# A two-layer graph kernel: sums over edges as 32-column products over four column groups, and a second product in two row halves

## The chip, the cores and the metric

The kernel runs on one core of one Trainium2 chip. The metric is the device time of the whole program in microseconds (us), the median of several runs. A single profiled execution gives the trace from which all durations below are read. The engines are named as in the profile: PE (TensorE, matrix products), PEld (its weight loads, which can overlap products), DVE (VectorE), ACT (ScalarE), POOL (GpSimd), SP (SyncE, which here only starts DMAs).

## What is computed

Two message-passing layers over the same graph of 6250 nodes and 200000 edges, the edges sorted by destination. All data is float32. A node has 64 scalars and 32 vectors of three components (160 numbers). Layer 0, cut to what matters (layer 1 adds one more message, `m_v3`, built from a cross product, and has a gate at the end):

```python
weight = silu(edge_length_embedded @ W_fc1) @ W_fc2      # per edge: 192 numbers (layer 1: 224)
gs, gv = x1s[edge_src], x1v[edge_src]                    # gather the source node's row
mid0a = w0 * gs * e_s                                    # 64 scalars
mid0b = w3 * (einsum('euc,ec->eu', gv, e_v) / sqrt3)     # 32 scalars
mid1a = w1[:, :, None] * gs[:, :, None] * e_v[:, None, :]   # 64 vectors
mid1b = w2[:, :, None] * gv * e_s[:, :, None]            # 32 vectors
agg = segment_sum(concat(...), edge_dst, num_segments=n) / sqrt(16)
# then linear mixes of agg per node, a residual and a layer norm
```

## The kernel before

**Tiling.** Edges are padded to 392 groups of 512; a group is four tiles (`TPG`) of 128 edges, one edge on each partition. The program has five stages: `setup_phase` (tables of window starts, scaled weights, node projections), `edge_phase` for layer 0, `layer0_nodes_phase` (50 tiles of 128 nodes), `edge_phase` for layer 1, and `layer1_nodes_phase` (50 tiles). Each edge phase writes out four groups by hand and loops 97 times over a body of four (`GPB`).

**Sums over edges.** Because the edges are sorted, the 512 destinations of a group nearly always lie in a window of 40 nodes (`WIN`). DVE makes `match`, for each edge a row of 40 zeros and a one at its destination; ACT multiplies that row by the edge's attributes, so that there are five rows of 40 for each edge (`which` 0 to 4: times e1, e2, e3, e0, and plain). DVE makes the messages (`msg`, `MW` columns per edge, 96 scalars and vectors per component). PE then multiplies: messages as the stationary operand, a match row as the moving one, and the result, message columns on the partitions and 40 window nodes in the free dimension, is summed in PSUM over the four tiles (`ps_sum`, up to four chunks of 40). DVE adds that window to `sums` in SBUF at the window's start (line 574). A group whose destinations span more than one window runs a loop of extra windows (lines 510 to 515 on PE).

**Who does what in one group.** On PE, the turn for group j is `hid(j)` (line 468, first product of the edge network), `edge_weights(j-1)` (line 479, second product, into `ps_w`) and `sum_group(j-2)` (line 489 in `window_sums`). ACT takes silu of `ps_h` (line 449) and scales the match rows (line 456). DVE runs `messages(j)` (lines 605 to 646), which needs `w_done` of that group and its gathered rows, then `add_group(j-1)`, which needs `sum_done`. POOL gathers the source rows: four indirect DMAs for each group (line 433), each for 128 edges, into four sets of `rows`; the gather of group j waits for the messages of group j-4. SP loads indices, network inputs and attributes, each in pairs of groups, in a fixed order with waits between them (lines 403 to 416).

**The layout that the change touches.** `window_sums` writes products of 64 message columns into partitions 0 to 63 or 64 to 127 and products of 32 columns into partitions 64 to 95 or 96 to 127. Per tile of edges that is, in layer 0, one product of 64 columns against 120 (three match rows), two of 64 against 40, and four of 32 against 40; layer 1 has two more of 64 against 40. PE splits each float32 product into two weight loads and two matmuls. In the placement before, the four groups of 32 partitions get 120, 120, 120 and 200 moving columns per tile in layer 0, and 160, 160, 160 and 240 in layer 1.

**Second product.** In layer 1 `hidden` holds two tiles of edges at once, 64 hidden values of each on partitions 0 to 63 and 64 to 127, and `fc2_1` is block diagonal (480 columns): one product with all 128 rows makes the weights of two tiles.

**Node phases.** `sums` is staged by ACT (lines 758, 892) and multiplied by `out0` or `out1`, whose columns repeat and zero-pad the weights to fit the mixed layout (lines 788 to 790 and 925 to 928). The order of work on each engine is as written; nothing is reordered by a planner.

## Time and profile before

| | us |
|---|---|
| median of 3 runs | 4755.46 |
| lowest, highest | 4745.83, 4756.82 |
| the profiled execution, from first to last instruction (its span) | 4749.6 |

In the span, setup takes until about 138 us, the edges of layer 0 until about 2165, the nodes of layer 0 until about 2387, the edges of layer 1 until about 4611, and the nodes of layer 1 the rest. The difference between span and median, 5.9 us, lies around the profiled instructions. A timeline row is one or several consecutive instructions, with the start of the first and the time until the end of the last; a row's end on PE is modelled, so a duration is best read from one row's start to the next row's start.

### The profile page before, as it was taken

The page shows a single profiled execution, that of the slowest core. Times are in us where ns is not written, and L with a number is a line of the kernel's source. Part 1 is how long each engine was busy: PE and PEld are TensorE (multiplying, and loading weights), DVE is VectorE, ACT ScalarE, POOL GpSimd, SP SyncE. Part 2 cuts the span into 40 slices and gives each one's busy share as a digit, 9 for nine tenths or more (in the row PEclk, how much of TensorE's full clock was granted, in tenths as well). Part 3 has the DMA queues.
Part 4 walks back from the last instruction along what each step waited for, and adds up shares of the span by engine and source line. Part 5 has one row for each costly group of instructions (what it writes and reads, how often), then busy time and mean ns, then how long its engine had stood idle before and what let it go on. Part 6 is the DMA issues. An engine that isn't in the chain of part 4 may idle for free. (4 is left out here: it accounts for less than half of the span.)

```text
span 4749.6 us, 166762 instructions
## 1 busy us (share of the span) xinstructions
PE 4615.8 (97%) x58000; PEld 3438.2 (72%) x58001; DVE 2968.4 (62%) x7746; ACT 2970.1 (63%) x12216; POOL 3050.4 (64%) x3215
## 2 busy tenths in 40 slices
PE   7899999999999999999889999999999999999996
PEld 4677777777777777776667777777777777777766
DVE  3455545454455445455767777777777777777768
ACT  1566666666666666663366676767676766666653
POOL 2677777777777777771266666666666666666641
PEclk9999999999999999999899999999999999999995
DMA  3222222222222222223343333333333333333333
GB/s 104 71 71 71 70 71 70 71 70 71 71 71 71 70 71 70 72 70 91 90 129 108 106 108 107 108 107 107 108 107 108 106 108 106 108 107 108 106 89 96
DMA packets 356348, 430.11 MB, mean 91 GB/s; under 512 B 203298, under 2 KB 248648, under 8 KB 356112
## 3 DMA queue, kind: packets, MB, share of 16 engines
q0 software_dynamic: 156288, 329.79, 25.4%
q1 hardware_dynamic: 199618, 98.11, 8.0%
q10 hardware_dynamic: 400, 1.68, 0.1%
q8 instruction: 23, 0.38, 0.0%
q14 instruction: 19, 0.16, 0.0%
HBM read 405.56 MB, written 23.74 MB: 90 GB/s over the span
## 5 line engine op out<-in xcount | busy, mean ns | idle before, releaser
L433 POOL DMA_INDIRECT e_rows<-scratch_table,e_index x3136 | 2963.7, 945 | 1305.2 <-issue 1209.6
L456 ACT ACTIVATE e_match<-e_match,e_attr 128x40 f32<-128x40 f32 x10976 | 2481.3, 315 | 237.7 <-DMA e_attr<-in_edge_attr 230.2
L489 PEld LDWEIGHTS e_sum<-e_match,e_msg 128*64 128x64 f32 (+1 forms) x50176 | 2102.4, 124 | 653.8 <-issue 363.7
L489 PE MATMUL e_sum<-e_match,e_msg 128*32 128x40 f32 (+2 forms) x50176 | 2486.3, 228 | 0.2 <-issue 0.2
L479 PE MATMUL e_w<-k_fc,e_hidden 100*128 100x192 f32 (+1 forms) x4704 | 1273.8, 407 | 0.0
L449 ACT ACTIVATE e_hidden<-e_h 100x512 f32<-100x512 f32 (+1 forms) x784 | 384.1, 490 | 1170.3 <-PE e_h L468 1170.2
L479 PEld LDWEIGHTS e_w<-k_fc,e_hidden 100*128 100x128 f32 (+1 forms) x4704 | 832.9, 191 | 384.4 <-issue 364.0
L574 DVE TENSOR_TENSOR sums<-sums,e_sum 128x120 f32 (+1 forms) x784 | 235.9, 301 | 947.9 <-PE e_sum L489 884.3
L635 DVE TENSOR_TENSOR e_msg<-e_w,e_rows 128x512 f32<-128x512 f32 x784 | 540.7, 690 | 451.3 <-PE e_w L479 437.5
L468 PE MATMUL e_h<-e_inputs,k_fc 128*100 128x512 f32 (+1 forms) x1568 | 709.9, 534 | 30.5 <-DMA e_inputs<-in_inputs 26.9
L641 DVE TENSOR_TENSOR e_msg<-e_w,e_rows 128x384 f32<-128x384 f32 x784 | 428.4, 546 | 0.0
L643 DVE TENSOR_TENSOR e_msg<-e_w,e_rows 128x384 f32<-128x384 f32 x784 | 428.1, 546 | 0.0
L554 DVE TENSOR_TENSOR e_match<-e_misc,e_dst_rel 128x160 f32<-128x160 f32 x788 | 252.4, 320 | 53.0 <-DMA e_dst_rel<-scratch_dst_rel 11.2
L468 PEld LDWEIGHTS e_h<-e_inputs,k_fc 128*100 128x100 f32 (+1 forms) x1568 | 216.2, 177 | 74.6 <-DMA e_inputs<-in_inputs 27.3
L625 DVE TENSOR_TENSOR e_misc<-e_misc,e_rows 128x384 f32<-128x384 f32 x392 | 218.0, 556 | 5.0 <-DMA e_rows<-scratch_table,e_index 4.5
L626 DVE TENSOR_TENSOR e_cross_b<-e_misc,e_rows 128x384 f32<-128x384 f32 x392 | 214.5, 547 | 0.0
L640 DVE TENSOR_TENSOR e_msg<-e_misc,e_cross_b 128x384 f32<-128x384 f32 x392 | 214.0, 546 | 0.0
L646 DVE TENSOR_TENSOR e_msg<-e_w,e_msg 128x384 f32<-128x384 f32 x392 | 213.6, 545 | 0.0
L605 DVE COPY e_misc<-e_attr 128x48 f32<-128x48 f32 x392 | 82.5, 211 | 134.3 <-issue 115.1
L618 DVE TENSOR_TENSOR e_match<-e_misc,e_match 128x160 f32<-128x160 f32 x392 | 124.2, 317 | 2.0 <-DVE e_match L554 0.2
L729 POOL DMA_DIRECT2D m_xv<-in_xT_v x10 | 5.4, 540 | 156.2 <-DVE m_y L822 140.3
L758 ACT ACTIVATE m_staged<-sums 128x384 f32 (+1 forms) x50 | 26.0, 523 | 86.9 <-PE m_agg L790 77.7
(122 smaller groups left out, 1440.8 us busy)
## 6 DMA issues: line engine op xcount, KB each, us to landing
e_rows<-scratch_table,e_index POOLq DMA_INDIRECT x3136
e_inputs<-in_inputs SPq DMA_DIRECT2D x196, 256.0 KB
e_attr<-in_edge_attr SPq DMA_DIRECT2D x392, 24.0 KB, 1.7
e_inputs<-in_inputs SPq DMA_DIRECT2D x196, 40.0 KB
e_index<-in_src SPq DMA_DIRECT2D x392, 4.0 KB, 1.9
scratch_self<-m_h SPq DMA_DIRECT2D x10, 480.0 KB, 4.7
f_self<-scratch_self POOLq DMA_DIRECT2D x10, 480.0 KB, 5.2
m_xrow<-in_x POOLq DMA_DIRECT2D x10, 400.0 KB, 4.9
```

What stands on the lines that cost most here:

```text
L433: pool.indirect_dma_start(out=rows[j][:, t, :], out_offset=None, in_=table_dram, in_offset=bass.IndirectOffsetOnAxis(ap=index[q][:, c:c + ...
L449: nc.scalar.activation(hidden[j % 2][:, :], ps_h[0:layer.hid, 0:layer.group_cols], ACT.Silu, scale=layer.silu_scale).then_inc(silu_done, 1)
L456: last = nc.scalar.activation(match[j][:, t, c, :], match[j][:, t, 4, :], ACT.Copy, scale=attr[q][:, e0 + t, e:e + 1])
L468: nc.tensor.matmul(ps_h[0:layer.hid, 0:n], w[f"fc1_{L}"][:, :], inputs[j // 2][:, (j % 2) * n:(j % 2) * n + n], start=True, stop=True).the ...
L479: last = nc.tensor.matmul(ps_w[j % 2][:, c0:c0 + n], hidden[j % 2][:, u * P:(u + 1) * P], w[f"fc2_{L}"][:, :], start=True, stop=True)
L489: return nc.tensor.matmul(out[rows, c0:c0 + n, :], m[:, t, f:f + rows.stop - rows.start], m5[:, t, which:which + n, :], start=(first and t ...
L554: return nc.vector.tensor_tensor(into[:, :, 4, :], iota_t, rel_of(g).unsqueeze(2).broadcast_to([P, TPG, WIN]), ALU.is_equal)
L574: nc.vector.tensor_tensor(at, at, window, ALU.add).then_inc(added, 1)
L625: nc.vector.tensor_tensor(comps(cross_a), e3(3), comps(r[:, :, 96:192]), ALU.mult)
L635: nc.vector.tensor_tensor(m[:, :, 0:128].rearrange("p t (k n) -> p t k n", k=2), wt[:, :, 0:128].rearrange("p t (k n) -> p t k n", k=2), r ...
L641: nc.vector.tensor_tensor(comps(m[:, :, 128:224]), w_v(128), comps(r[:, :, 64:160]), ALU.mult)
L643: last = nc.vector.tensor_tensor(comps(m[:, :, 224:320]), w_v(160), comps(r[:, :, 64:160]), ALU.mult)
```

## The change

- `window_sums` now makes only products of 32 message columns, 10 per tile in layer 0 and 13 in layer 1, on a layout in which each chunk of `sums` holds one vector component (chunks 0 to 2) or the scalars (chunk 3). The moving columns per group of 32 partitions and tile become 160, 160, 120, 120 in layer 0 and 160, 160, 160, 200 in layer 1. `first` is set on one product per partition group only. In layer 0, DVE zeroes `ps_sum` once, and PE waits for that.
- Both layers use all four chunks, so layer 0's window add is 160 wide instead of 120, its staging 512 instead of 384, and the clearing of `sums` after layer 0 covers four chunks instead of three.
- The second product of layer 1 is four products of 64 rows by 224 columns instead of two of 128 rows by 480; `inputs1` is laid out so that the two row halves write different PSUM banks.
- `out0` and `out1` lose the padding: layer 0's nodes use three products of 64 columns and one of 128 (before 320, 128 and 192), layer 1's three of 32 and one of 96 (before 192, 64, 128 and 96). Setup has fewer products and scalings, and the five warm-up products per edge phase have 224 columns instead of 480.

```diff
@@ edge_weights
+                fc2, n = w[f"fc2_{L}"], layer.wn
                 for u in range(TPG // layer.tiles_per_product):
-                    c0, n = u * layer.tiles_per_product * WPITCH, w[f"fc2_{L}"].shape[1]
-                    last = nc.tensor.matmul(ps_w[j % 2][:, c0:c0 + n], hidden[j % 2][:, u * P:(u + 1) * P], w[f"fc2_{L}"][:, :],
-                                            start=True, stop=True)
+                    for h in range(layer.tiles_per_product):
+                        c0, k = (u + 2 * h) * WPITCH, fc2.shape[0] // layer.tiles_per_product
+                        last = nc.tensor.matmul(ps_w[j % 2][:, c0:c0 + n], hidden[j % 2][k * h:k * h + k, u * P:(u + 1) * P],
+                                                fc2[k * h:k * h + k, :], start=True, stop=True)
@@ window_sums
-                    product(slice(0, 64), 0, 64, 0, n=3, first=True, end=(L == 0))
-                    product(slice(64, 128), 2, 0, 3, first=True)
-                    product(slice(64, 128), 0, 128, 3)
-                    product(slice(64, 96), 1, 192, 3, end=(L == 0))
-                    for c in range(3):
-                        last = product(slice(96, 128), 1, 224 + V * c, c, end=(L == 0 and c == 2))
-                    if L == 1:
-                        product(slice(0, 64), 3, 320, 4, end=True)
-                        last = product(slice(64, 128), 3, 384, 4, end=True)
+                    product(0, 0, 64, 0, n=3, first=True)
+                    product(1, 0, 96, 0, n=3, first=True)
+                    product(2, 0, 128, 3, first=True)
+                    product(3, 3, 224, 0, first=True)
+                    product(2, 1, 160, 3)
+                    product(3, 3, 256, 1)
+                    product(0, 3, 0, 3, end=True)
+                    product(1, 3, 32, 3, end=True)
+                    if L == 0:
+                        product(2, 2, 192, 3, end=True)
+                        last = product(3, 3, 288, 2, end=True)
+                    else:
+                        product(2, 2, 192, 3)
+                        product(3, 0, 320, 4)
+                        product(2, 3, 288, 2, end=True)
+                        product(3, 1, 352, 4)
+                        last = product(3, 2, 384, 4, end=True)
@@ add_group
-                window = ps_sum[j % 2][:, 0:layer.chunks, :]
+                window = ps_sum[j % 2]
...
-                at = sums[:, 0:layer.chunks, bass.ds(start, WIN)]
+                at = sums[:, :, bass.ds(start, WIN)]
@@ layer 0 nodes, output
-                nc.tensor.matmul(agg, staged[b][:, 1, :], w["out0"][:, 0:320], start=True, stop=False)
-                nc.tensor.matmul(agg[:, :, 0:64], staged[b][:, 0, :], w["out0"][:, 320:448], start=False, stop=False)
-                nc.tensor.matmul(agg[:, :, 64:160], staged[b][:, 2, :], w["out0"][:, 448:640], start=False,
-                                 stop=True).then_inc(out_mm, 1)
+                for c in range(3):
+                    nc.tensor.matmul(agg[:, :, V * c:V * c + V], staged[b][0:MID, c, :], w["out0"][0:MID, 0:2 * V], start=True, stop=True)
+                nc.tensor.matmul(agg[:, :, V3:D], staged[b][:, 3, :], w["out0"][:, 2 * V:192], start=True, stop=True).then_inc(out_mm, 1)
```

How it stands on PE. In layer 1, one group, before (`e_h` is `hid`, `e_w` is `edge_weights`, `e_sum` is `window_sums`; a shape is output partitions by columns; the first two tiles of the four):

```order
L468 MATMUL e_h<-e_inputs,k_fc_1 128x256
L479 MATMUL e_w<-k_fc_1,e_hidden 128x480 x2
L505 TENSOR_LOAD k_table
L505 ISA x2
L489 MATMUL e_sum<-e_match,e_msg 64x120
L489 MATMUL e_sum<-e_match,e_msg 64x40 x2
L489 MATMUL e_sum<-e_match,e_msg 32x40 x4
L489 MATMUL e_sum<-e_match,e_msg 64x40 x2
L489 MATMUL e_sum<-e_match,e_msg 64x120
L489 MATMUL e_sum<-e_match,e_msg 64x40 x2
L489 MATMUL e_sum<-e_match,e_msg 32x40 x4
```

and now:

```order
L440 MATMUL e_h<-e_inputs,k_fc_1 128x256
L453 MATMUL e_w<-k_fc_1,e_hidden 128x224 x4
L487 TENSOR_LOAD k_table
L487 ISA x2
L463 MATMUL e_sum<-e_match,e_msg 32x120 x2
L463 MATMUL e_sum<-e_match,e_msg 32x40 x11
L463 MATMUL e_sum<-e_match,e_msg 32x120 x2
L463 MATMUL e_sum<-e_match,e_msg 32x40 x11
```

The turn keeps its order; the sums no longer alternate between 64 and 32 columns, and have 52 products per group where they had 36. In layer 0 they have 40 where they had 28.

At the start of layer 0's nodes, two node tiles before (`m_self` is the residual part, `m_agg` the part from `sums`):

```order
L785 MATMUL m_self<-k_node_v,m_xv 128x2x96
L786 MATMUL m_self<-k_node_s,m_xs 128x2x64
L788 MATMUL m_agg<-k_out,m_staged 128x320
L789 MATMUL m_agg<-k_out,m_staged 128x2x64
L790 MATMUL m_agg<-k_out,m_staged 128x2x96
L785 MATMUL m_self<-k_node_v,m_xv 128x2x96
```

and now:

```order
L770 MATMUL m_self<-k_node_v,m_xv 128x2x96
L771 MATMUL m_self<-k_node_s,m_xs 128x2x64
L774 MATMUL m_agg<-k_out,m_staged 128x2x32 x3
L775 MATMUL m_agg<-k_out,m_staged 128x2x64
L770 MATMUL m_self<-k_node_v,m_xv 128x2x96
```

Three products became four, with half the columns in all (320 for 640).

## Rows read from the trace of the kernel before

**Rows 1.** A stretch: length; busy us (instructions) of PE, PEld, DVE, ACT, POOL; clock, DMA.
```profile
3600.00:4000.00 400.00, 400.00 (x5538) 284.83 (x5538) 297.98 (x710) 279.86 (x1211) 268.04 (x284) 1.00 0.39 107
```

**Rows 2.** Timeline of PE, layer 0: start, us, instructions, count.
```profile
1504.59 1.47 PE L479 MATMUL e_w<-k_fc,e_hidden 100*128 100x192 f32 x8
1505.98 2.87 PE L489 MATMUL e_sum<-e_match,e_msg 128*64 128x120 f32 x56
1508.78 0.67 PE L468 MATMUL e_h<-e_inputs,k_fc 128*100 128x512 f32 x1
```

**Rows 3.** Timeline of PE, layer 1.
```profile
3000.06 0.70 PE L468 MATMUL e_h<-e_inputs,k_fc 128*128 128x256 f32 x2
3000.60 1.77 PE L479 MATMUL e_w<-k_fc,e_hidden 128*128 128x480 f32 x4
3002.30 3.47 PE L489 MATMUL e_sum<-e_match,e_msg 128*64 128x120 f32 x72
3005.70 0.70 PE L468 MATMUL e_h<-e_inputs,k_fc 128*128 128x256 f32 x2
```

**Rows 4.** Line 433 by phase: count, ns min/median/max, first to last start.
```profile
L433 POOL DMA_INDIRECT e_rows<-scratch_table,e_index x1568: 940/946/1020, 138.4 to 2148.2; - x196
L433 POOL DMA_INDIRECT e_rows<-scratch_table,e_index x1568: 940/946/1010, 2389.3 to 4590.8; - x196
```

**Rows 5.** Timeline of POOL, layer 1: in brackets the idle time before.
```profile
3006.34 0.95 POOL L433 DMA_INDIRECT e_rows<-scratch_table,e_index  x1 [0.30 <-issue]
3007.59 0.95 POOL L433 DMA_INDIRECT e_rows<-scratch_table,e_index  x1 [0.30 <-issue]
```

**Rows 6.** Stretches, weight loads of line 489 alone, one layer-1 tile: length, busy (count).
```profile
3003.00:3003.43 0.43, 0.43 (x10) 1.00 1.01 363
3003.43:3003.47 0.04, 0.00 (x0) 1.00 0.95 378
3003.48:3003.77 0.29, 0.28 (x8) 1.00 0.74 269
```

**Rows 7.** The page, groups of instructions: count, busy us, mean ns, idle before.
```profile
L489 PE MATMUL e_sum<-e_match,e_msg 128*32 128x40 f32 (+2 forms) x50176 | 2486.3, 228 | 0.2 <-issue 0.2
```

**Rows 8.** Timeline of DVE, layer 1, two groups.
```profile
3000.43 0.32 DVE L574 TENSOR_TENSOR sums<-sums,e_sum 128x160 f32 x1 [1.11 <-PE e_sum L489]
...
3004.41 0.54 DVE L646 TENSOR_TENSOR e_msg<-e_w,e_msg 128x384 f32<-128x384 f32 x1
3006.07 0.32 DVE L574 TENSOR_TENSOR sums<-sums,e_sum 128x160 f32 x1 [1.11 <-PE e_sum L489]
...
3010.37 0.55 DVE L646 TENSOR_TENSOR e_msg<-e_w,e_msg 128x384 f32<-128x384 f32 x1
```

**Rows 9.** Timeline of DVE: the last window add of each edge phase.
```profile
2163.76 0.28 DVE L574 TENSOR_TENSOR sums<-sums,e_sum 128x120 f32 x1 [2.67 <-PE e_sum L489]
...
4610.12 0.32 DVE L574 TENSOR_TENSOR sums<-sums,e_sum 128x160 f32 x1 [3.11 <-PE e_sum L489]
```

**Rows 10.** Timelines of PE and of DVE, nodes of layer 0.
```profile
2282.03 0.81 PE L788 MATMUL m_agg<-k_out,m_staged 128*128 128x320 f32 x2
...
2285.41 0.81 PE L788 MATMUL m_agg<-k_out,m_staged 128*128 128x320 f32 x2
...
2280.37 0.38 DVE L822 SCALAR_TENSOR_TENSOR m_y<-m_self,k_attr,m_xrow 128x160 f32<-128x160 f32 x1
...
2283.55 0.38 DVE L822 SCALAR_TENSOR_TENSOR m_y<-m_self,k_attr,m_xrow 128x160 f32<-128x160 f32 x1
```

**Rows 11.** A stretch in the nodes of layer 1, columns as in rows 1.
```profile
4620.00:4700.00 80.00, 69.03 (x284) 62.23 (x282) 65.86 (x309) 30.63 (x102) 11.28 (x13) 0.61 0.23 68
```

**Rows 12.** Timeline of PE as layer 1's edges begin.
```profile
2391.82 1.22 PE L468 MATMUL e_h<-e_inputs,k_fc 128*128 128x256 f32 x2 [0.47 <-ACT e_hidden L449]
```

**Rows 13.** The page: an instruction queue (packets, MB); the index loads (last: landing).
```profile
q8 instruction: 23, 0.38, 0.0%
...
e_index<-in_src SPq DMA_DIRECT2D x392, 4.0 KB, 1.9
```

More of the change, by code:

```diff
@@ L62 @@
 WPITCH = 256
-MW = 448
+MW = 416
 WARM_UP = 5
@@ L246, in _ @@
             pe.wait_ge(l_in, 32)
-            for c in range(16):
-                vec = c not in (6, 7, 14, 15)
-                col = OUT0_COLUMNS[c] + (64 if c >= 12 else 0)
-                n = V if vec else S
-                last = nc.tensor.matmul(ps_out[:, col:col + n], l2[:, c, :], l3[:, S:S + V] if vec else l3[:, 0:S],
-                                        start=True, stop=True)
+            for k in range(2):
+                nc.tensor.matmul(ps_out[:, V * k:V * k + V], l2[:, k, :], l3[:, S:S + V], start=True, stop=True)
+            for k in range(2):
+                c0 = 2 * V + S * k
+                last = nc.tensor.matmul(ps_out[:, c0:c0 + S], l2[:, 2 + k, :], l3[:, 0:S], start=True, stop=True)
             last.then_inc(out0_done, 1)
@@ L487, in window_sums, with product @@
                 for t in range(TPG):
-                    def product(rows, c0, f, which, n=1, first=False, end=False):
-                        return nc.tensor.matmul(out[rows, c0:c0 + n, :], m[:, t, f:f + rows.stop - rows.start],
+                    def product(g, c0, f, which, n=1, first=False, end=False):
+                        return nc.tensor.matmul(out[32 * g:32 * g + 32, c0:c0 + n, :], m[:, t, f:f + 32],
                                                 m5[:, t, which:which + n, :], start=(first and t == 0),
                                                 stop=(end and t == TPG - 1))
-                    product(slice(0, 64), 0, 64, 0, n=3, first=True, end=(L == 0))
-                    product(slice(64, 128), 2, 0, 3, first=True)
-                    product(slice(64, 128), 0, 128, 3)
-                    product(slice(64, 96), 1, 192, 3, end=(L == 0))
-                    for c in range(3):
-                        last = product(slice(96, 128), 1, 224 + V * c, c, end=(L == 0 and c == 2))
-                    if L == 1:
-                        product(slice(0, 64), 3, 320, 4, end=True)
-                        last = product(slice(64, 128), 3, 384, 4, end=True)
+                    product(0, 0, 64, 0, n=3, first=True)
[15 more added lines that the diff above has]
+                        last = product(3, 2, 384, 4, end=True)
                 return last
@@ L524, in _ @@
             for c in range(WARM_UP):
-                nc.tensor.matmul(ps_h[:, 0:480], w["ident"][:, :], w["out1"][:, :], start=True, stop=True)
+                nc.tensor.matmul(ps_h[:, 0:224], w["ident"][:, :], w["fc2_1"][:, :], start=True, stop=True)
             with pe.Fori(1, BODIES) as i:
@@ L539, in _ @@
                     nc.vector.memset(inputs[q][:, :], 0.0).then_inc(zeroed, 1)
-            for b in range(2):
-                nc.vector.memset(msg[b][:, :, 416:448], 0.0)
+            if L == 0:
+                for b in range(2):
+                    nc.vector.memset(ps_sum[b], 0.0).then_inc(zeroed, 1)
             nc.vector.memset(dst_rel[:, T:T + AHEAD * TPG], 0.0)
@@ L592, in add_group @@
                             skip_runtime_bounds_check_because="extras count the whole windows up to a destination below NPAD")
-                        at = sums[:, 0:layer.chunks, bass.ds(there, WIN)]
+                        at = sums[:, :, bass.ds(there, WIN)]
                         nc.vector.tensor_tensor(at, at, window, ALU.add).then_inc(x_added, 1)
@@ L681, in layer0_nodes_phase @@
         h1 = [sb(f"h1_{s}", [P, TPU, R1]) for s in range(UPB)]
-        staged = [sb(f"staged{b}", [P, 3, P]) for b in range(2)]
+        staged = [sb(f"staged{b}", [P, 4, P]) for b in range(2)]
         y = [[sb(f"y{b}_{c}", [P, D]) for c in range(4)] for b in range(2)]
@@ L733, in _ @@
             pool.wait_ge(stage_done, NT)
-            nc.gpsimd.memset(sums[:, 0:3, :], 0.0)
+            nc.gpsimd.memset(sums[:, :, :], 0.0)
         @block.sync
@@ L757, in stage @@
                 at_least(act, out_mm, n - 1)
-                nc.scalar.activation(staged[b][:, :, :], sums[:, 0:3, bass.ds(n * P, P)], ACT.Copy).then_inc(stage_done, 1)
+                nc.scalar.activation(staged[b][:, :, :], sums[:, :, bass.ds(n * P, P)], ACT.Copy).then_inc(stage_done, 1)
             def deviation(n, i, s, k, b):
@@ L924, in output @@
                 o = ps[b]
-                nc.tensor.matmul(o[:, 0:O1], staged[b][:, 1, :], w["out1"][:, 0:192], start=True, stop=False)
-                nc.tensor.matmul(o[:, 0:64], staged[b][:, 0, :], w["out1"][:, 192:256], start=False, stop=False)
-                nc.tensor.matmul(o[:, 64:O1], staged[b][:, 2, :], w["out1"][:, 256:384], start=False, stop=False)
-                nc.tensor.matmul(o[:, 0:V3], staged[b][:, 3, :], w["out1"][:, 384:480], start=False, stop=True).then_inc(out_mm, 1)
+                for c in range(3):
+                    nc.tensor.matmul(o[:, V * c:V * c + V], staged[b][:, c, :], w["out1"][:, 0:V], start=True, stop=True)
+                nc.tensor.matmul(o[:, V3:O1], staged[b][:, 3, :], w["out1"][:, V:V + S1], start=True, stop=True).then_inc(out_mm, 1)
             node_loop(pe, output)
```

51 lines of the change are left out of this document (19 added, 32 removed).

## The prediction, made before the changed kernel ran

> **What bounds the kernel now.** I read the busy times by stretch first, then the timelines of PE and POOL, then who waits. In both edge phases PE never rests: in 400 us of layer 1 it is busy for 400, while DVE has 298, ACT 280 and POOL 268 [rows 1]. The edge phases are what counts: from the first gather to the last window add they take 2163.8 - 138.4 and 4610.1 - 2389.3, together 4246 of the 4750 us [rows 4, 9]. One group on PE takes, in layer 0, 1.39 for the second product, 2.80 for the sums and the rest of 5.13, 0.94, for the first [rows 2, 4]; in layer 1 it is 0.54, 1.70 and 3.40, so 5.64 [rows 3]. The next limit stands close behind. Where POOL has nothing to wait for, its gathers start 1.25 us apart (0.95 of work, 0.30 of issue) [rows 5], and a group has four: 5.00 us. The gathers of one phase run from 138.4 to 2148.2 and from 2389.3 to 4590.8 [rows 4]; over 1567 steps of one gather that is 5.13 and 5.62 per group, so PE holds POOL back by 0.13 and 0.62. A gain on PE beyond these two amounts is not seen in the time. There are no extra windows on this data: 50176 matmuls on line 489 are 392 x (56 + 72) exactly [rows 2, 3, 7].
>
> **The sums.** The change takes away the alternation of 64 and 32 columns and adds products: 40 for 28 in layer 0, 52 for 36 in layer 1, two matmuls each. Is a product of 32 columns beside others in other column groups nearly free, or does it queue? The price of a moving column comes from the second product of layer 1: 4 matmuls of 480 columns in 1.70 us, 0.885 ns each [rows 3]. The stretch of one tile in layer 1 begins with ten loads for matmuls of 280 x 2 = 560 columns in 64-column form, and 0.48 us after its start the first load of the 32-column form begins [rows 6]. One after another these columns would take 0.496 us, with no time for the first load or the 0.04 in which nothing is loaded. So products on the two halves of the columns do run side by side. If they do fully, the columns explain only (160 + 120) x 2 x 0.885 = 0.50 of a tile's 0.85 us in layer 1 and 0.42 of 0.70 in layer 0: the other 0.28 to 0.35 lies at the two changes of form in each tile, where the array empties and the first weights load uncovered. Those go.
>
> Ends for the new sums. Low: four groups side by side, bounded by the fullest: 160 columns x 2 x 0.885 x 4 tiles = 1.13 in layer 0 and 200 in its place, 1.42, in layer 1, plus 0.1 to enter. High: no two ever overlap and each matmul follows at the pace of the eight loads of 32 columns, 0.29 / 8 = 0.036 [rows 6]: 80 x 0.036 = 2.9 and 104 x 0.036 = 3.8. Between them, with two groups side by side as the row shows, (560 x 2 x 0.885 x 4) / 2 = 1.98 and (680 x ...) / 2 = 2.41. I take 2.0 and 2.4, since two abreast is what a row shows and four is only the same thing carried on.
>
> A rule speaks against products this small. The Trainium skill, "TensorEngine Tiling (Array Packing)", section "Instruction Overhead", says that a matmul costs about 60 cycles whatever its columns, so that one should not cut a dimension that is already small; "TensorE: Matmul & The Clock Gate" puts the floor at 25 ns from start to start. By that the sums would be 2.0 and 2.6 us, and the low end could not be reached; no row here goes below 36 ns over a run of eight. The time forecast would be the same.
>
> **The second product of layer 1.** 2 products of 480 columns become 4 of 224. Serially: 8 matmuls x 224 x 0.885 = 1.59; if the row halves run side by side, 0.80. No row shows two row halves at once, so both ends stay, each with one change of form, 0.1 to 0.2. I take 1.3. Nobody downstream minds: DVE waits for w_done once per group.
>
> **PE after the change.** Layer 0: 0.94 + 1.39 + 2.0 = 4.3 (3.6 to 5.2). Layer 1: 0.54 + 1.3 + 2.4 = 4.2 (2.9 to 5.9). Both centres lie below POOL's 5.00, so **POOL becomes the bound** in both layers. What then is late next? DVE in layer 1: from one window add to the end of line 646 is 4.52 without the attribute copies (3000.43 to 3004.95, a 0.32 wait for PE in it) and 4.85 with them (3006.07 to 3010.92) [rows 8], 4.7 in the mean, and some 0.2 to pass from the last message to the next add: 4.9 at most, under 5.00 by little. ACT has 280 of 400 us at 5.63 per group, 3.9 [rows 1]. The add in layer 0 grows by a third to the 0.32 of layer 1 [rows 8, 9], under slack. SP's loads wait for gathers, first products and sums of groups long past; with POOL as the bound the sums of a group end some two turns after its gather, and the indices were asked for before that, so I cost its order at nothing. It has about one pair of groups of cover.
>
> **The sum.** Gathers of layer 0: 1567 x 1.25 = 1958.8 for 2009.8: -51.0. Layer 1: 1958.8 for 2201.5: -242.7. Tails from the last gather's start to the last add: before 15.6 and 19.3, because POOL was groups ahead [rows 4, 9]. Now POOL is last, and what follows it is its own 0.95, the landing, one group of messages and one of sums: I estimate 9 and 10.5, so -7 and -9. Nodes of layer 0: a turn is 3.38 on PE and 3.18 on DVE [rows 10]; the new products have half the columns, so at most DVE's 3.18 is reached, 50 x 0.2 = 10 at best, nothing at worst (four products need two more loads of 128 columns); I take -5. ACT's wider staging and POOL's longer clearing lie beside the stores that end that phase. Nodes of layer 1: DVE is busy for 66 of 80 us and PE waits for ACT, so 0 [rows 11]. Setup loses seven short scalings: -1. Total -316. Against the profiled execution: 4749.6 - 316 = 4434. The median of the runs stands 5.9 above that span, so **4440 us**, 6.6% faster.
>
> **Rivals.**
>
> *Column groups do not overlap as I think* (the slower side). If all products ran in sequence, column by column, the sums would be 560 x 2 x 0.885 x 4 = 3.97 and 4.81: PE at 6.30 and, with the serial second product, 6.94 per group, or 392 x (1.17 + 1.32) = +980, 5730 us. Against it: the 0.48 us for 560 columns [rows 6]. At the pace of one matmul per 0.036 instead, PE has 5.2 and 5.1 to 5.9: 4550 to 4900. It decides where the two groups together pass 5.13 + 5.62. Chance 0.03 each.
>
> *The loop no longer stays in PE's instruction store* (slower too). The trace: one instruction queue brought 23 packets, 0.38 MB, in the whole run [rows 13], though each edge loop ran 97 times; so the loops were not fetched again. Counting two loads and two matmuls per product and the copy of the sums for extra windows, layer 1's loop body grows from 4 x (3 + 72) x 4 = 1200 to 4 x (5 + 104) x 4 = 1744 instructions, beside a few dozen of control, half as much again, and nothing shows that this still fits. The Trainium skill, "Runtime: NRT & Kernel Launch", section "Instruction fetch mechanics", says that TensorE's store holds 2048 instructions in blocks of 256 and that a taken branch to a block that is not there waits for a DMA. By that the new body, some 1800 instructions in eight or nine blocks, just fits or just doesn't. The price from this kernel: the 23 packets are 16.5 KB each, the whole program, so the body of layer 1 was some 5 of them and is now some 7. No row prices a packet that is waited for; the nearest is the landing of a small load, 1.9 us [rows 13]. One per body, at the jump back, is 0.5 per group, and PE's 4.2 hides it under 5.00. All seven, waited for every time, would be 7 x 1.9 / 4 = 3.3 per group: PE at 7.5 in layer 1, 4440 + 392 x 2.5 = 5420. Against no change it decides at 5.9 per group, 1.7 us of fetching. Chance of that 0.04.
>
> *The clock.* PE will rest for 15 to 30% of each turn. Through the edge phases the granted clock is 1.00 with PE always busy [rows 1]; in the nodes of layer 1, where PE stands before 11 of 80 us and works in short bursts, it is 0.61, mostly the 1.2 GHz level [rows 11]. At that level the first product of layer 1 takes 1.22 for 0.70 [rows 12, 3]; all of PE's 4.2 would be about 7. That would at once make PE busy without rest, as now, so it can't last; a third of the time low gives 5.1 per group on average, +40 to +80: 4500. Chance 0.10.
>
> *DVE and PE hand over late in layer 1.* DVE's 4.9 is near 5.00; with one wait of 0.3 for PE per group it binds at 5.2: +80, 4520. It speaks against this that w_done and the sums come a turn ahead once PE is faster. Chance 0.10.
>
> *Sums bound as before because the layout gains nothing*: then layer 0 stays, and layer 1 gains its second product alone, 392 x 0.4: 4600. Chance 0.02.
>
> **How the numbers follow.** Forecast 0.68, clock 0.10, DVE 0.10, the rest 0.12. A measurement of this kernel tells 0.3%, 14 us, from no change. Slower by more: 0.08 (serial, fetch, and part of the 0.036 case); within: 0.01; faster: 0.91. The low end: POOL's 5.00 is firm, tails and nodes can give 15 more: 4422. The high end takes in the clock and DVE cases: 4550.
>
> **What would show it.** In the trace after: gathers 1.25 apart throughout, last starts near 2097 and 4285; POOL the engine without idle time, PE with waits for DVE of 0.5 to 1.5 per group; sums of line 463 in 1.2 to 2.6 us with no gap between loads inside a group; second product between 0.8 and 1.7; granted clock 1.00; instruction packets near 31, not thousands. Wrong would be: gathers further apart than 1.25 with DVE or PE as the releaser, or a clock below 1 in the loops.

## The result, and the profile after

The changed kernel takes **5733.9 us** (median of 4 runs, 5727.5 to 5736.8) beside 4752.9 for the kernel before in the same session: a ratio of 1.206, 95% interval 1.204 to 1.208. It is 20.6% slower, where 6.6% faster was forecast. Its profiled execution has a span of 5729.4 us.

The page of the kernel after shows in three lines where to look: busy time by engine, the clock in 40 slices, and an instruction queue (packets, MB, share).

```profile
PE 3761.5 (66%) x81596; PEld 2835.8 (49%) x81597; DVE 2912.3 (51%) x7737; ACT 2951.2 (52%) x12216; POOL 3055.4 (53%) x3215
...
PEclk9999999999999985577777777777777777777775
...
q8 instruction: 895, 14.66, 1.1%
```

PE works less than before in all (3761.5 us busy for 4615.8), and yet every engine waits. The queue that had brought 23 packets [rows 13] brings 895. The gathers by phase (line 405 is line 433 of before) say when:

```profile
L405 POOL DMA_INDIRECT e_rows<-scratch_table,e_index x1568: 942/946/1020, 136.9 to 2095.1; - x196
L405 POOL DMA_INDIRECT e_rows<-scratch_table,e_index x1568: 940/946/1005, 2423.0 to 5562.3; - x196
```

Layer 0 went from 2009.8 us to 1958.2, as forecast. Layer 1 went from 2201.5 to 3139.3, which is 8.01 us per group in place of 5.62 [rows 4]. PE's timeline over one turn of layer 1's loop (four groups), from one first product to the same one of the next turn:

```profile
4002.03 1.22 PE L440 MATMUL e_h<-e_inputs,k_fc 128*128 128x256 f32 x2 [9.11 <-issue]
4003.18 1.87 PE L453 MATMUL e_w<-k_fc,e_hidden 64*128 64x224 f32 x8
4004.97 2.89 PE L463 MATMUL e_sum<-e_match,e_msg 128*32 128x120 f32 x104
4009.93 0.69 PE L440 MATMUL e_h<-e_inputs,k_fc 128*128 128x256 f32 x2 [2.06 <-issue]
...
4017.27 1.76 PE L463 MATMUL e_sum<-e_match,e_msg 128*32 128x40 f32 x96 [0.70 <-issue]
4021.39 0.97 PE L440 MATMUL e_h<-e_inputs,k_fc 128*128 128x256 f32 x2 [2.36 <-issue]
...
4034.38 1.22 PE L440 MATMUL e_h<-e_inputs,k_fc 128*128 128x256 f32 x2 [8.18 <-issue]
```

Each gap in brackets is put down to "issue": PE waits for nothing that another engine or a transfer of data would release. The products themselves are short. The DMA queues of 32 us of the same stretch show what arrives meanwhile, nine packets in one turn:

```profile
q8 instruction: 9, 0.15, 2.2%
```

With the same stretches as before, layer 0, the node stage and layer 1 (columns as in rows 1):

```profile
1500.00:1900.00 400.00, 305.76 (x7229) 231.06 (x7220) 195.19 (x563) 260.02 (x1044) 302.47 (x320) 1.00 0.28 73
2140.00:2360.00 220.00, 220.00 (x757) 170.10 (x756) 98.80 (x337) 60.19 (x189) 13.95 (x21) 0.50 0.26 73
3600.00:4000.00 400.00, 218.61 (x5586) 163.01 (x5586) 205.46 (x494) 191.74 (x836) 189.63 (x202) 0.75 0.30 80
```

In layer 1 PE is busy for 219 of 400 us, against 400 of 400 [rows 1]. It rests for 14.5 of each turn's 32 us; shared out over the nine packets that is 1.6 us each in the mean. That the rests are waits for these packets is inferred here, and tested below. The second line holds another loss: in the node stage after layer 0 the clock is 0.50, its 1.2 GHz level, and PE never rests, while in the middle of that stage before it had

```profile
2190.00:2370.00 180.00, 159.54 (x791) 117.91 (x791) 129.48 (x400) 65.42 (x220) 32.14 (x25) 0.90 0.38 105
```

The sum by phase, in us, read from the gathers and the spans (e1 and e16 are the experiments of that number; the forecast column has the predicted differences from before, and -12 is -7 for the tail of layer 0's edges and -5 for the nodes):

| | before | after | e1 | e16 | forecast |
|---|---|---|---|---|---|
| to the first gather | 138.4 | 136.9 | 136.7 | 136.9 | -1 |
| gathers of layer 0 | 2009.8 | 1958.2 | 1958.7 | 1958.9 | -51.0 |
| to the next first gather (nodes) | 241.1 | 327.9 | 327.7 | 242.9 | -12 |
| gathers of layer 1 | 2201.5 | 3139.3 | 1958.6 | 1958.6 | -242.7 |
| to the end | 158.8 | 167.1 | 151.9 | 152.1 | -9 |
| span | 4749.6 | 5729.4 | 4533.6 | 4449.4 | -316, to 4434 |

### The profile page after: what moved, and what is told of

It reads as the page before. It is cut to its first block and busy times, and to the rows that moved or that the text cites. A ratio compares the mean times of both kernels' runs of the same rounds, so it can differ in the third digit from the quotient of the medians.

```text
span 5729.4 us, 213946 instructions
## 1 busy us (share of the span) xinstructions
PE 3761.5 (66%) x81596; PEld 2835.8 (49%) x81597; DVE 2912.3 (51%) x7737; ACT 2951.2 (52%) x12216; POOL 3055.4 (53%) x3215
## 3 DMA queue, kind: packets, MB, share of 16 engines
q8 instruction: 895, 14.66, 1.1%
## 5 line engine op out<-in xcount | busy, mean ns | idle before, releaser
L463 PE MATMUL e_sum<-e_match,e_msg 128*32 128x40 f32 (+1 forms) x72128 | 1454.6, 234 | 518.5 <-DVE e_msg L628 389.0
L463 PEld LDWEIGHTS e_sum<-e_match,e_msg 128*32 128x32 f32 x72128 | 1310.2, 123 | 844.8 <-issue 426.6
L440 PE MATMUL e_h<-e_inputs,k_fc 128*100 128x512 f32 (+1 forms) x1568 | 794.6, 593 | 1349.0 <-issue 1298.1
L453 PE MATMUL e_w<-k_fc,e_hidden 100*128 100x192 f32 (+1 forms) x6272 | 1155.4, 415 | 3.1 <-issue 3.1
L453 PEld LDWEIGHTS e_w<-k_fc,e_hidden 100*128 100x128 f32 (+1 forms) x6272 | 904.7, 223 | 397.8 <-issue 384.5
L440 PEld LDWEIGHTS e_h<-e_inputs,k_fc 128*100 128x100 f32 (+1 forms) x1568 | 250.5, 203 | 1442.5 <-issue 1405.6
L559 DVE TENSOR_TENSOR sums<-sums,e_sum 128x160 f32 x784 | 246.3, 314 | 140.9 <-PE e_sum L463 132.6
L743 ACT ACTIVATE m_staged<-sums 128x512 f32 (+1 forms) x50 | 31.4, 629 | 156.3 <-PE m_agg L775 140.4
```

What stands on the lines that cost most here:

```text
L440: nc.tensor.matmul(ps_h[0:layer.hid, 0:n], w[f"fc1_{L}"][:, :], inputs[j // 2][:, (j % 2) * n:(j % 2) * n + n], start=True, stop=True).the ...
L453: last = nc.tensor.matmul(ps_w[j % 2][:, c0:c0 + n], hidden[j % 2][k * h:k * h + k, u * P:(u + 1) * P], fc2[k * h:k * h + k, :], start=Tru ...
L463: return nc.tensor.matmul(out[32 * g:32 * g + 32, c0:c0 + n, :], m[:, t, f:f + 32], m5[:, t, which:which + n, :], start=(first and t == 0) ...
L559: nc.vector.tensor_tensor(at, at, window, ALU.add).then_inc(added, 1)
```

## The experiments

**Theory A:** layer 1's loop on PE no longer fits into the engine's instruction store, so all of it is fetched again in every turn. Counted in the programs, with four instructions for a 32-bit product, its body has 1276 instructions before and 1820 after; nearly half is the copy of the sums for windows beyond the 40 nodes, which stands in every group and never runs on this data. All instruction counts below are made in this way and come from no trace; blocks are the 256 instructions of the rule that the prediction quotes, and one packet of the queue is 14.66 MB / 895 = 16.4 KB. **Theory B:** the products of 32 columns, or the handover between PE and DVE, are slow in layer 1's mix.

**e1_compact** shortens what is not executed, and **e2_before_padded** lengthens it in the kernel before.

```diff
-                    with pe.Fori(0, extras) as x:
-                        pe.wait_ge(x_matched, before + x + 1)
-                        window_sums(j, match_x).then_inc(x_sum_done, 1)
+                    with pe.Fori(0, extras * TPG) as x:
+                        pe.wait_ge(x_matched, before * TPG + x + 1)
+                        window_sums(j, msg_t, match_t, 1).then_inc(x_sum_done, 1)
```

> The changed kernel with one thing rewritten: the branch for destinations beyond the 40-node window (never taken on this data) holds the products of one tile in place of four, with a loop around them and a VectorE copy of the tile in front. What is executed on this data stays the same. PE's loop body in layer 1 falls from 1820 instructions to 1196 (before the change: 1276), counting four for a product of 32-bit data. Theory A, the loop no longer fits into PE's instruction store: the instruction queue has fewer than 60 packets, not 895, and layer 1 goes at POOL's 5.00 us per group, so that 3139 us between its first and last gather become about 1965 and the total is 5734 - 1175 = about 4560 us (4530 to 4640). Rival B, the 32-column products or the handover of data between PE and VectorE are what costs 8.0 us per group: the branch isn't executed, and the time stays at 5734 (5700 to 5760).

Measured: **4536.0 us** (4534.9 to 4536.4), ratio 0.955 (0.953 to 0.956). Packets, gathers of layer 1, and two turns of PE:

```profile
q8 instruction: 22, 0.36, 0.0%
```
```profile
L406 POOL DMA_INDIRECT e_rows<-scratch_table,e_index x1568: 942/946/1010, 2423.1 to 4381.7; - x196
```
```profile
3500.29 0.69 PE L441 MATMUL e_h<-e_inputs,k_fc 128*128 128x256 f32 x2 [0.51 <-issue]
3500.91 1.03 PE L454 MATMUL e_w<-k_fc,e_hidden 64*128 64x224 f32 x8
3503.18 1.65 PE L462 MATMUL e_sum<-e_match,e_msg 128*32 128x120 f32 x104 [1.25 <-DVE e_msg L634]
3504.85 0.69 PE L441 MATMUL e_h<-e_inputs,k_fc 128*128 128x256 f32 x2
```

The executed products are the same, and the time is 1198 us less. Layer 1 runs at POOL's 5.00 us per group, and PE waits for DVE in each group, as the forecast had it. Theory B is gone: the products of 32 columns and their handover are all still there.

e2 adds to each of the four branches of layer 1's loop in the kernel before:

```diff
                 with pe.If(extras):
+                    for _ in range(34):
+                        nc.tensor.matmul(ps_sum[j % 2][0:64, 3, :], msg[j % 2][:, 0, 320:384], match[j][:, 0, 4, :],
+                                         start=True, stop=True)
```

> The kernel before the change, with 34 products (136 instructions) added inside each of the four never-taken branches of layer 1's loop on PE, so that its body has 1820 instructions like the changed one, in place of 1276. Nothing more is executed. Theory A (instruction store): some 9 packets of instructions per loop body, near 900 in all, and layer 1 at 7.2 to 9.2 us per group in place of 5.62, so 4753 + 388 x 2.4 = about 5680 us (5350 to 6150). Rival B (the new products or the new handover): the padding is never executed, 4753 us (4735 to 4770).

Measured: **6072.9 us**, ratio 1.278 (1.276 to 1.280), 889 packets, and layer 1 at 8.98 us per group:

```profile
q8 instruction: 889, 14.57, 1.1%
```
```profile
L433 POOL DMA_INDIRECT e_rows<-scratch_table,e_index x1568: 940/946/1010, 2395.9 to 5915.6; - x196
```

Instructions that never run cost the old kernel 28%. The central estimate was too low (5680), the bounds held. A group has 2.5 us of rest (PE stands before line 468 for 112.2 us in the stretch from 3600 to 4000), and its products take 6.5 us in place of 5.6, since the clock there is 0.83 where it was 1.00 [rows 1].

**e3_one_gap** asks whether the length of the loop counts or the blocks it touches; the padding is that of e2, 206 products in a single branch of e1.

> e1_compact with 206 products (824 instructions) added inside one of the four never-taken branches of layer 1's loop: the body is 2020 instructions long, longer than the changed kernel's 1820, but 886 of them are passed by in one jump, so that PE touches 6 blocks of 256 instructions, and 8 with the block behind each stretch. Theory A1, what counts is the blocks that are fetched: it fits, under 60 packets, and the time is that of e1_compact. Theory A2, what counts is the length of the loop from its first to its last instruction: about 9 packets per body and 8 us per group or more, 5650 us or more.

Measured: 4536.5 us, 23 packets. A body of 2020 instructions, longer than the changed kernel's 1820, costs nothing when 886 of them are jumped over at once. So the distance from the first to the last instruction doesn't decide; this fits with what was expected if only the blocks that PE passes through, and the one behind each such stretch, are fetched.

**e5_fits, e6_shifted, e9_shifted_again, e14_shifted_healthy** look for the edge. e5 pads e1 by 29 products in each branch; e6 is e5 with 33 more ahead of the loop:

```diff
+            if L == 1:
+                never = pe.value_load(w["table"][0:1, 0:1, 1:2], min_val=0, max_val=NPAD // WIN - 1)
+                with pe.If(never):
+                    for _ in range(33):
+                        nc.tensor.matmul(ps_h[:, 0:224], w["ident"][:, :], w["fc2_1"][:, :], start=True, stop=True)
```

> e1_compact with 29 products (116 instructions) added inside each of the four never-taken branches of layer 1's loop: the body has 1660 instructions and reaches over 7 blocks of 256 instructions (8 with the one fetched behind it). Theory A, nine blocks per turn of the loop don't fit and eight do: under 60 instruction packets, the time of e1_compact, 4536 us (4525 to 4550). Rival A3, the store holds fewer (or the time grows with each instruction that is passed by): between 4600 and 5700 us.

> e5_fits with 33 products more in another never-taken branch ahead of layer 1's loop, which is passed once: the loop is the same 1660 instructions, but begins 137 instructions later, so that it reaches over 8 blocks of 256 (9 with the one behind). Theory A: near 900 instruction packets, and layer 1 at 7.5 us per group or more, 5500 us or more, for the same body as e5_fits. Rival A4, only the length of the body counts: the time of e5_fits, 4536 us.

> The kernel of e6_shifted once more, beside a kernel before that runs at its 4750 us: 1660 instructions per turn of layer 1's loop, 137 of padding passed once ahead of it, so that the loop reaches over 8 blocks of 256 instructions in place of 7. Theory A: near 900 instruction packets again (888 in e6_shifted, 24 in e5_fits), layer 1 at 7.2 us per group or more, and 5400 us or more. Rival A4, the packets come ahead of need and cost little: within 100 us of e1_compact's 4536.

> The kernel of e6_shifted (layer 1's loop of 1660 instructions, begun 137 later than in e5_fits, so that it reaches over 8 blocks of 256), on another chip. Theory A: near 888 instruction packets as in its two runs so far, layer 1 at 7.2 us per group or more, 5400 us or more beside a kernel before at 4750 us. Rival A4: the packets come ahead of need where PE gets its instructions in time otherwise, within 100 us of 4536.

The chip of e5 to e8 and that of e9 to e12 ran the kernel before itself in 8083 and 8078 us, so times from these eight are only set against runs of the same chip. Measured there: e5 7861.5 us with 24 packets, e6 8354.4 us with 888; e9 8345.2 us with 888. The packets answer the question: the same 1660 instructions per turn, begun 137 later, change 24 packets into 888, and on the same chip the time grows by 6.3%. On a chip with the kernel before at 4753 us the shifted kernel takes **5693.1 us** (ratio 1.198, 1.195 to 1.200):

```profile
q8 instruction: 888, 14.55, 1.2%
```
```profile
L406 POOL DMA_INDIRECT e_rows<-scratch_table,e_index x1568: 940/946/1010, 2422.3 to 5525.2; - x196
```

So the price is a step. By the count, a turn of the loop that reaches over seven blocks, eight with the one fetched behind them, runs free; where it reaches over eight, nine with that one, all nine come again. The packets agree to the last one: by the same count the whole programs have 31 full blocks after the change, 25 in e2 and 24 in e14 (23 in the kernel before and 22 in e1, as their queues brought), and 895 - 31, 889 - 25 and 888 - 24 are each 864, nine for each of the 96 jumps back of the 97 turns. Where exactly seven blocks end depends on the hand count; that a shift by 137 instructions makes the difference does not. e5's own time on a chip at 4753 us was not run; e1 and e3, with as few packets, stand for it.

**e15_halves_healthy** (first run as e8_halves_alone and e11_halves_alone) does one part alone in the kernel before; **e18_layout_alone** does the other: e1 with this edit taken back.

```diff
-                    last = nc.tensor.matmul(ps_w[j % 2][:, c0:c0 + n], hidden[j % 2][:, u * P:(u + 1) * P], w[f"fc2_{L}"][:, :],
-                                            start=True, stop=True)
+                    for h in range(layer.tiles_per_product):
+                        c0, k = (u + 2 * h) * WPITCH, fc2.shape[0] // layer.tiles_per_product
+                        last = nc.tensor.matmul(ps_w[j % 2][:, c0:c0 + n], hidden[j % 2][k * h:k * h + k, u * P:(u + 1) * P],
+                                                fc2[k * h:k * h + k, :], start=True, stop=True)
```

> The kernel before the change with the second product of layer 1 in two row halves alone; the sums and everything behind them stay as they were. In e1_compact the eight half products take 1.03 us per group, against 1.70 before [rows 3]. PE's turn in layer 1 of 5.62 us then falls to 4.95, just under POOL's 5.00 per group: layer 1 at 5.00, and 4752 - 392 x 0.62 = about 4510 us (4500 to 4545). Rival: the halves save less beside the old sums, PE stays last and the time is between 4545 and 4650 us; layer 0 is as before in either case.

> The kernel of e8_halves_alone once more, beside a kernel before that runs at its 4750 us: the kernel before with the second product of layer 1 in two row halves alone. In e1_compact the eight half products take 1.03 us per group against 1.70 before [rows 3]: PE's turn in layer 1 falls to 4.95 us, under POOL's 5.00, and the total to 4752 - 392 x 0.62 = about 4510 us (4500 to 4545). Rival: the halves save less beside the old sums, PE stays last in layer 1, 4545 to 4650 us.

> The kernel of e8_halves_alone (before, with the second product of layer 1 in two row halves alone), on another chip. PE's turn in layer 1 falls by 1.70 - 1.03 us to 4.95, under POOL's 5.00 per group: 4752 - 392 x 0.62 = about 4510 us (4500 to 4545). Rival: the halves save less beside the old sums, 4545 to 4650 us.

> e1_compact with the second product of layer 1 as it was before the change (one product for two tiles, against a block-diagonal 128 x 480), so that only the layout of the sums is new, in a loop that fits. PE's turn in layer 1 is then 0.62 + 1.70 [rows 3] + 1.7 for the sums = 4.0 us, under POOL's 5.00: 4536 us as e1_compact (4520 to 4550). Rival: the two parts need each other, and layer 1 stands above 5.1 us per group: 4575 us or more.

Measured: e15 **4510.7 us** (ratio 0.948, 0.947 to 0.950), e18 **4535.8 us** (0.954, 0.953 to 0.956). e15's PE timeline:

```profile
3503.52 0.70 PE L467 MATMUL e_h<-e_inputs,k_fc 128*128 128x256 f32 x2
3504.15 1.03 PE L480 MATMUL e_w<-k_fc,e_hidden 64*128 64x224 f32 x8
3505.11 3.47 PE L490 MATMUL e_sum<-e_match,e_msg 128*64 128x120 f32 x72
3508.51 0.70 PE L467 MATMUL e_h<-e_inputs,k_fc 128*128 128x256 f32 x2
```

A turn is 4.99 us, and the second product takes 0.96 from start to start where it took 1.70 [rows 3]. Either part alone brings layer 1 to POOL's pace, e15 with PE still busy without rest; the change did both. e15 stands below e1 and e18 in the total because it keeps the old node stage after layer 0 (247.8 us from last to first gather for e1's 327.7); layer 0 itself gains only by the new layout (2009.5 in e15, 1958.7 in e1). On the two chips at 8080 us the halves alone were 1.9% and 2.0% slower than before (8240.4 and 8232.2 us), a sign that does not carry over and that was not followed up.

**The node stage after layer 0.** e1 leaves one term of the forecast open, 87 us here. In it the three products of 64 columns on 96 rows (and one of 128) have taken the place of three of 320, 128 and 192, and the clock stays at 0.50. Seven kernels, each with its edit on top of e1:

```diff
 e4:
-                    nc.tensor.matmul(agg[:, :, V * c:V * c + V], staged[b][0:MID, c, :], w["out0"][0:MID, 0:2 * V], start=True, stop=True)
+                    nc.tensor.matmul(agg[:, :, V * c:V * c + V], staged[b][:, c, :], w["out0"][:, 0:2 * V], start=True, stop=True)
 e7, e13, e16, e17, ahead of the stage:
+            for _ in range(24):
+                nc.tensor.matmul(ps_next[1][:, 0:224], w["ident"][:, :], w["fc2_1"][:, :], start=True, stop=True)
 e10 and e13 once, e12 twice before a tile's transposes; e16 once, e17 twice before its first product on the staged sums:
+                    nc.tensor.matmul(ps_tr[b][:, 0:384], w["ident"][0:V3, :], w["node_v0"][:, :], start=True, stop=True)
```

> e1_compact with the three 64-column products of the node stage after layer 0 taken over all 128 rows of the staged tile in place of 96 (the 32 more rows are zeros, the sum is unchanged). The stage took 328 us between layer 0's last and layer 1's first gather against 241 before, at a granted clock of 0.50 against 0.80 to 1.00. Theory C, the number of rows in use decides whether the clock is raised: clock near 1.00 in the stage, 241 to 260 us for it, 70 to 85 us less than e1_compact. Rival D, it is the columns per time (many products of 64 columns, of which each takes longer than its columns): the rows change nothing, clock 0.50 and the time of e1_compact within 5 us.

> e1_compact with 24 unused products of 128 x 224 on PE ahead of the node stage after layer 0, so that its first real products find PE at the full clock. Theory E, the stage holds the full clock once it has it: the stage's clock is 1.00 and it takes 240 to 260 us in place of 328, the total 4536 - 75 = about 4460 us (4445 to 4480). Rival F, with its mix of products the stage falls back to 0.50 of the clock by itself: no gain, and up to 15 us more for the unused products, 4530 to 4555 us.

> e1_compact with one unused product of 128 x 384 per node tile in the node stage after layer 0, on top of its fourteen. In e7_warm_nodes the stage lost the full clock again 10 to 15 us after it had it, with PE busy throughout, so that the mix is suspected: a tile of it has 640 columns in 3.36 us in its first six products at the low clock, against 960 columns in 3.95 us before. Theory G, a product of many columns per tile brings the clock back: 1.00 in the stage, 240 to 262 us for it in place of 328, and 4536 - 75 = about 4460 us (4445 to 4480). Rival H, the stage stays at 0.50 and pays for the products, 50 times 1.3 us: about 4600 us (4580 to 4620).

> As e10_dense_nodes with two such unused products per tile. Theory G: if one was not enough, two are; if one was, the second costs nothing as long as VectorE is what the stage waits for at the full clock: 4460 us (4445 to 4490). Rival H: 0.50 and 50 times 2.6 us more than e1_compact, about 4665 us (4630 to 4690).

> e1_compact with both aids in the node stage after layer 0: 24 unused products of 128 x 224 ahead of it and one unused product of 128 x 384 per tile. e7_warm_nodes alone lost the full clock after 10 to 15 us, e10_dense_nodes never got it, e12_dense_twice got it after 30 us and kept it. Theory G (a tile's columns decide, and fewer are enough to keep the clock than to raise it): 1.00 of the clock from the stage's first tiles on, the stage 245 to 265 us in place of 328, and 4536 - 72 = about 4465 us (4450 to 4485). Rival H: one per tile doesn't keep it, the stage falls to 0.50 and takes 395 to 410 us as in e10: about 4610 us.

> e1_compact with 24 unused products of 128 x 224 ahead of the node stage after layer 0 and one unused product of 128 x 384 in the first step of each tile (in e13 it stood in a later step, so that the first tiles of the stage went without it). Theory G: the full clock stays from the first tile on, the stage takes 245 to 265 us in place of 328, 4536 - 72 = about 4465 us (4450 to 4485). Rival H: one wide product per tile is too little at the full clock as well, the stage falls to 0.50 and takes 400 us: about 4605 us.

> As e16_wide_first with two such products per tile. In e12 a tile took 4.44 us with two of them at the full clock, so 50 tiles take 222 us, and with filling and draining the stage takes about 255: 4536 - 73 = about 4463 us (4450 to 4490) if the clock holds. If it falls all the same, e12 shows that it comes back after some 30 us: 4480 to 4500.

| | last to first gather, us | total, us | beside before at |
|---|---|---|---|
| e1 | 327.7 | 4536.0 | 4751 |
| e4 | 327.5 | 4535.7 | 4751 |
| e7 | 338.5 | 7883.2 | 8083 |
| e10 | 401.8 | 7943.4 | 8078 |
| e12 | 296.2 | 7826.9 | 8078 |
| e13 | 386.8 | 4597.0 | 4753 |
| e16 | 242.9 | **4451.1** | 4752 |
| e17 | 274.4 | 4482.7 | 4752 |

e7, e10 and e12 ran on the two chips at 8080 us; there the same stage without any aid takes 340.0 (e5, the chip of e7) and 340.6 us (e9, the chip of e10 and e12). The rows used are indifferent (e4). In e7 the stage gets the full clock from the products ahead of it and has lost it within 10 us. PE had just rested twice, 0.32 us for DVE and 0.79 for ACT; from then on it is busy without rest, and the clock does not come back:

```profile
3795.00:3805.00 10.00, 10.00 (x57) 9.65 (x56) 0.00 (x0) 0.19 (x1) 3.60 (x6) 1.00 0.65 166
3815.00:3950.00 135.00, 135.00 (x467) 104.59 (x466) 64.47 (x221) 37.12 (x118) 9.98 (x15) 0.50 0.28 78
```

In e10 one wide product per tile leaves the clock at 0.50 throughout. In e12 two per tile raise it by themselves (0.50 from 3780 to 3800, 1.00 from 3820 on, PE busy all the time) and keep it. In e13 the stage starts at the full clock, but its first tiles, while the pipeline fills, go without the wide product; after a rest of 0.32 us for DVE at 2122.4 the clock falls, and it is 0.50 for good. e16 has the same number of unused products with the wide one in each tile's first step, and keeps the clock:

```profile
2120.00:2140.00 20.00, 20.00 (x116) 15.00 (x115) 17.79 (x63) 8.80 (x23) 2.00 (x3) 1.00 0.23 61
2140.00:2360.00 220.00, 191.08 (x1228) 142.86 (x1229) 143.66 (x427) 87.91 (x297) 51.67 (x39) 0.89 0.38 108
```

In every 20 us from 2140 to 2300 of e16 the clock is 1.00 and PE is busy throughout; the 0.89 comes from the end of the stage, behind the last products. The stage is within 2 us of its old 241, and e16 is the fastest kernel of the study: 0.936 of before (0.935 to 0.938). e17's second product only adds work for PE. That the half clock is what costs the 87 us is shown: with more products than e1 and the full clock the stage is back at its old length. Why the clock holds or falls is not settled. The width of the products is one candidate, and for e7 and e13 against e16 there is another that no run separates from it: the rest just before the fall, which e16, with more for PE to do per tile, doesn't have in its first tiles.

## Why the prediction was wrong

**The failed step is the instruction-store rival: an overflow was taken to cost one packet or so per turn, and all of them at every turn was given 0.04.** The prediction named this mechanism, counted the body at 1744 instructions "beside a few dozen of control", and said that some 1800, "in eight or nine blocks, just fits or just doesn't". Then it priced the same body as 7 packets, showed that one per turn would be hidden, and gave no reason for the small chance of the rest. The runs show no such mild case: the packets are nine per jump back or none (888 in all in e6, 24 in e5), and layer 1 takes 8.01 us per group in place of the forecast 5.00. The count could have said more beforehand: 1820 instructions are more than seven times 256, so the body reaches over at least eight blocks wherever it begins, while the body of before, 1276, reached over six, and no row showed that more than that run free. The rule that was quoted, the Trainium skill, "Runtime: NRT & Kernel Launch", section "Instruction fetch mechanics", has 2048 instructions in blocks of 256, eight blocks; by the count, e5 and e14 agree with that (eight blocks with the one behind run free, nine don't). By that rule alone the forecast should have been near an even chance between 4440 and its rival.

**The rival's own price was too low.** It had 7 packets of 1.9 us, 3.3 us per group, on top of a PE turn of 4.2: 7.5, 5420 us. Measured are 9 packets of 1.6 us of rest, 3.6 per group, and a PE that is busy for 4.4 per group in place of e1's 3.5, at a clock of 0.75 in place of 0.97: 8.0 and 5734 us. The two blocks too few are the eighth and the one fetched behind, and the lower clock was not in the price at all.

**The sums** were taken as two abreast, 2.0 and 2.4 us. They take 1.4 (layer 0: 1504.55 to 1505.95 in the trace after) and 1.67 from start to start in e1's layer 1, near the low ends of 1.13 + 0.1 and 1.42 + 0.1. One after another the columns of layer 1 are 4.81 us; in 1.67 us that is 2.9 abreast in the mean, so more than two groups of columns run together. The row that was held to show two abreast showed a lower bound. That is 104 matmuls in 1.67 us, 16 ns each. As an estimate from the pages, the Trainium skill's floor of 25 ns from start to start ("TensorE: Matmul & The Clock Gate", section "Wait — 56ns, not 53.3ns?") and the Trainium skill's 60 cycles per matmul ("TensorEngine Tiling (Array Packing)", section "Instruction Overhead") would make it 2.6 us; where page and row differ, the row decides. **The second product** takes 0.96 to 1.03, not 1.3 and far from the serial 1.59, so two row halves do run side by side.

**POOL as the bound** held: 5.00 us per group in layer 0 after the change and in both layers of e1, 1958.2 to 1958.9 us for the forecast 1958.8. **DVE** was not late: e1's gathers stay 1.25 apart through layer 1. **The tail** after layer 1 was right once the loop fitted (-6.9 for -9). That a gain on PE past POOL's pace is not seen in the time was right too: e15 and e18 have half of the change each and layer 1 at the same 5.00.

**The node stage** was costed at -5 from the turns at full clock [rows 10], with "half the columns" as a gain. With the tail before it, where -12 was forecast, +87 was measured, since the clock was an input of that sum and the change moved it. The clock rival looked for this in the edge loops, where e1 has 1.00 and 0.97, and not in the node stage. Its argument that a low clock makes PE busy without rest and so "can't last" is refuted there: PE is busy for 220 of 220 us at 0.50.

The forecast of 4440 is 11 us from e16, which repairs both losses; as a forecast of the changed kernel it was wrong by 1294 us. Even the 11 us flatter it: the spans differ by 15 (4434 and 4449.4), 14 of it in the node stage, and the 5.9 us put between span and median were partly chance of the runs. In the changed kernel a run's own time is 2.1 us above its span (5731.5 and 5729.4).

## What to carry to other kernels

Before costing a change that unrolls more instructions into a hardware loop, count the body in the built program and see over how many blocks it reaches. Branches that never run count if they are short, as the copies of some 200 instructions here; a single one of 886 did not. Close to the edge the time is a step, 20% here, and even the place where the loop begins decides. Move rare code out of the loop or fold it into a small inner loop. And check that an engine's clock stays what it was before using durations taken at that clock: a stage in which PE is never idle can still run at half of it.

## What the runs showed of the hardware that was not expected

The step itself: one block too many brings all nine, at each jump back, with up to 9.1 us of rest at a single place of the turn and 1.6 us per block in the mean, while e5's turn, one block shorter by the count, fetches none.

A second thing has nothing to do with the change. On two chips the kernel before took 8080 us in place of 4750, and PE's timeline there has rests between single products, here from e7 in layer 0, in the middle of one group's sums:

```profile
3002.20 0.26 PE L462 MATMUL e_sum<-e_match,e_msg 128*32 128x40 f32 x3 [1.13 <-issue]
3003.64 0.22 PE L462 MATMUL e_sum<-e_match,e_msg 128*32 128x40 f32 x1 [1.18 <-issue]
3005.05 0.23 PE L462 MATMUL e_sum<-e_match,e_msg 128*32 128x40 f32 x1 [1.19 <-issue]
```

The instruction queue has its usual 22 packets there, so these rests are no fetches of the kind above. Their cause is open; that PE gets its instructions late on those chips is only what "issue" suggests.
